# A decoder layer on one core: VectorE instead of GpSimd normalises blocks 2 and 3 in the middle of the expert stage, and their turns, logits and routing stand one or two units earlier

## The chip, the cores and the metric

The kernel runs on one core of a Trainium2 chip. The time is device microseconds (us) of one launch, and lower is better. Engines are named as in the profile: PE (TensorE matmuls), DVE (VectorE), ACT (ScalarE), POOL (GpSimd), SP (SyncE, which starts transfers).

## The reference, cut to what matters

The input is 16 rows of 128 tokens with 256 features. Three sublayers follow one another, each with a residual sum and a layer norm: a selective state-space mixer, a cross attention, and a mixture of experts (8 routed experts, 2 chosen for each token, and a shared one).

```python
def _layernorm(x, axis=-1, eps=1e-05):
    m = jnp.mean(x, axis=axis, keepdims=True)
    v = jnp.var(x, axis=axis, keepdims=True)
    return (x - m) / jnp.sqrt(v + eps)

scores = jax.nn.sigmoid((xt @ gate.T).astype(jnp.float32))
_, sel = jax.lax.top_k(scores + expert_bias[None, :], TOP_K)
...
h = jax.nn.silu(xb @ w1e.T) * (xb @ w3e.T)
oe = (h @ w2e.T).astype(routed.dtype)
...
x = _layernorm(x + _L0_attn_ref(x, L0_attn_W_in, ...), axis=-1)
x = _layernorm(x + _L0_xattn_ref(x, ctx_512, ctx_512), axis=-1)
x = _layernorm(x + _L0_ffn_ref(x, L0_ffn_gate, L0_ffn_expert_bias, ...), axis=-1)
```

## The kernel before

The tokens lie in `acc` (128 partitions, 16 batch rows, 256 features). Four batch rows make a **block**; there are blocks 0 to 3. The change lies in the last stage, the experts, which begins while the attention of the last rows still runs.

Each engine has its own written order of instructions, and semaphores tie them together. The expert stage walks through the list `users`: 32 **units** (`u`, half of the experts for one batch row, so that units 0 to 15 are blocks 0 and 1, and units 16 to 31 blocks 2 and 3) and four shared steps S0 to S3, one for each block. S1 stands behind unit 3, S2 behind unit 11, S3 behind unit 19. For one unit the work goes round the engines like this:

- PE `expert_up(u)`: four matmuls, two for `w_up` and two for `w_gate`, into two PSUM banks (L1661).
- ACT `silu_unit(u)`: four activations (L1301). DVE `gate_unit(u)`: four products into `hid` (L1461).
- PE `turn_hidden(u)`: four transposes (L1668), which wait for DVE's products of that unit. In PE's order they stand behind `expert_up(u+1)`. ACT `evac_hidden(u)` copies them out (L1307).
- PE `down(u)`: the matmuls into the output bank (L1687; for an even unit three more of the shared expert, L1683). In PE's order it stands behind `turn_hidden(u+1)`. After two units DVE adds the row (`add_row`, L1467), and after four it takes the moments for the last norm (L1472, L1477, L1480).

A shared step is twelve matmuls on PE (`shared_up`, L1647), one activation (L1293), one product on DVE (`gate_shared`, L1451), and a split in two float16 parts on POOL (`split_hidden`, L1164 and L1166).

Before a block can be used in this stage, its rows must pass the second layer norm (moments on DVE, an inverse root on POOL (L1132), the normalisation itself), then be transposed by PE (`turn_x`, L1620, two steps of eight transposes for a block in all), be copied out by ACT (L1259), and be split and cast by POOL (`split_x`, L1158 and L1160, and `cast_x`, L1179). The router follows: `logits` on PE (L1628), a copy on ACT (L1263), `turn_logits` on PE (L1635), tanh on ACT (L1267), and on DVE the steps `bias_scores`, `find_best`, `take_best`, `find_best`, `take_best`, `set_weights` (L1397 to L1417), small instructions that each wait for the one before. Unit 16 is the first that needs the second half's weights. The table `asides` says behind which unit the turns (`("x", i)`), the logits and their transposes of blocks 2 and 3 stand, on PE and on ACT; a chain of `if` in DVE's loop says behind which unit the norm and routing steps stand. The last layer norm's rows are normalised by POOL too (`finish`, L1171 and L1175).

DVE normalises blocks 0 and 1 here (`norm_part` with parts 3 and 4, L1760), and all blocks of the first layer norm in the mixer stage. Blocks 2 and 3 are normalised by POOL in `normalise_block` (L1185).

Of the kernel before, what the change touches and what calls it, by code (L numbers as in the profile page):

```python
# [15 lines left out]
ALU = mybir.AluOpType  # L16
# [9 lines left out]
KT = DM // P  # L26
# [4 lines left out]
TB = 4  # L31
TOK = BATCH // TB * L
NB = BATCH // TB
# [8 lines left out]
def makers(nc, ctx):  # L42

    names = {}

    def sb(name, shape, dt):
        return ctx.enter_context(nc.sbuf_tensor(name, shape, dt))

    def ps(name, shape, dt=F32):
        return ctx.enter_context(nc.psum_tensor(name, shape, dt))  # L50

    def sem(name):
        if name not in names:
            names[name] = ctx.enter_context(nc.semaphore(name))
        return names[name]

    return sb, ps, sem
# [886 lines left out]
def attention_and_experts(nc, io, acc, moments, heads, small, w_up, w_gate, w_down):  # L944
# [7 lines left out]
    with ExitStack() as ctx:  # L952
        sb, ps, sem = makers(nc, ctx)
# [6 lines left out]
        mean_var, rstd, expo = moments  # L960
# [64 lines left out]


        users = ["S0"] + list(range(4)) + ["S1"] + list(range(4, 12)) + ["S2"] + list(range(12, 20)) + ["S3"] + list(range(20, UNITS))
        asides = {4: [("x", 4), ("x", 5)], 8: [("x", 6), ("x", 7)], 9: [("logits", 1), ("turned", 1)]}
        turns = []
        for u in range(UNITS):  # L1030
            turns += [("hidden", u - 1)] * (u > 0) + asides.get(u, [])
# [76 lines left out]
        def _(pool):  # L1108
# [14 lines left out]
            def add_heads(b, t):  # L1123
                pool.wait_ge(sem("att"), 2 * b + t + 2)
                x = acc[:, bass.ds(b, 1), t * P:t * P + P]
                nc.gpsimd.tensor_tensor(x, x, att[:, t].unsqueeze(1), ALU.add).then_inc(sem("x_add"), 1)  # L1126

            def inverse_root(t):

                pool.wait_ge(sem("ln_var"), t + 1)  # L1130
                r = rstd[:, t * NB:t * NB + NB]
                nc.gpsimd.tensor_tensor(r, r, expo[:, 0:NB], ALU.pow).then_inc(sem("ln_rstd"), 1)  # L1132
# [23 lines left out]
            def split_x(t):  # L1156
                pool.wait_ge(sem("xt"), KT * t + KT)
                nc.gpsimd.tensor_copy(x_parts[:, 0, :, t, :], xt[:, :, t, :]).then_inc(sem("x_split"), 1)  # L1158
                pool.wait_ge(sem("x_split"), 2 * t + 1)
                nc.gpsimd.tensor_tensor(x_parts[:, 1, :, t, :], xt[:, :, t, :], x_parts[:, 0, :, t, :], ALU.subtract).then_inc(sem("x_split"), 1)  # L1160

            def split_hidden(t):
                pool.wait_ge(sem("shared_hid"), t + 1)
                nc.gpsimd.tensor_copy(hid_parts[:, 0, t], hid_s[:, t % 2]).then_inc(sem("hid_hi"), 1)  # L1164
                pool.wait_ge(sem("hid_hi"), t + 1)
                nc.gpsimd.tensor_tensor(hid_parts[:, 1, t], hid_s[:, t % 2], hid_parts[:, 0, t], ALU.subtract).then_inc(sem("hid_lo"), 1)  # L1166

            def finish(i):
                r = rstd3[:, finals[i][0]:finals[i][-1] + 1]
                pool.wait_ge(sem("ln3_var"), i + 1)  # L1170
                nc.gpsimd.tensor_tensor(r, r, expo[:, 0:len(finals[i])], ALU.pow).then_inc(sem("ln3_rstd"), 1)  # L1171
                if len(finals[i]) > 1:
                    pool.wait_ge(sem("ln3_rstd"), i + 1)
                    for b in finals[i]:
                        nc.gpsimd.tensor_scalar(acc[:, b], acc[:, b], mean_var3[:, b, 0:1], rstd3[:, b:b + 1], ALU.subtract, ALU.mult).then_inc(sem("final"), 1)  # L1175

            def cast_x(t):
                pool.wait_ge(sem("xt"), KT * t + KT)
                nc.gpsimd.tensor_copy(xb[:, :, t, :], xt[:, :, t, :]).then_inc(sem("xb"), 1)  # L1179

            def normalise_block(t):
                pool.wait_ge(sem("ln_mean"), t + 1)
                pool.wait_ge(sem("ln_rstd"), t + 1)
                for b in range(NB * t, NB * t + NB):
                    nc.gpsimd.tensor_scalar(acc[:, b], acc[:, b], mean_var[:, b, 0:1], rstd[:, b:b + 1], ALU.subtract, ALU.mult).then_inc(sem("pool_x"), 1)  # L1185

            add_heads(BATCH - 3, 0)
            add_heads(BATCH - 3, 1)
            inverse_root(0)
# [7 lines left out]
            add_heads(BATCH - 1, 1)  # L1197
            split_hidden(0)
            split_x(1)
            normalise_block(2)  # L1200
            split_hidden(1)
            cast_x(1)
            inverse_root(3)
            normalise_block(3)
            split_x(2)
            cast_x(2)
            finish(0)
            finish(1)
            split_hidden(2)
            split_x(3)  # L1210
            cast_x(3)
            finish(2)
            finish(3)
            split_hidden(3)
# [110 lines left out]
        def _(dve):  # L1325
# [57 lines left out]
            def routed(ins):  # L1383

                steps[0] += 1
                ins.then_inc(sem("route"), 1)
                dve.wait_ge(sem("route"), steps[0])
# [3 lines left out]
            def blocks(half):  # L1391
                return slice(HALF * half, HALF * half + HALF)

            def bias_scores(half):
                r = blocks(half)
                dve.wait_ge(sem("score"), half + 1)
                routed(nc.vector.tensor_scalar(score[:, r], score[:, r], 0.5, 0.5, ALU.mult, ALU.add))  # L1397
                routed(nc.vector.tensor_tensor(biased[:, r], score[:, r], ebias[:].unsqueeze(1).broadcast_to(full), ALU.add))

            def find_best(half):  # L1400
                r = blocks(half)
                routed(nc.vector.tensor_reduce(best[:, r], biased[:, r], AX.X, ALU.max))
                routed(nc.vector.tensor_tensor(equal[:, r], biased[:, r], best[:, r].unsqueeze(2).broadcast_to(full), ALU.is_equal))

                routed(nc.vector.tensor_tensor(equal[:, r], equal[:, r], earlier[:].unsqueeze(1).broadcast_to(full), ALU.mult))

            def take_best(half, i):
                r = blocks(half)
                routed(nc.vector.tensor_reduce(nearest[:, r], equal[:, r], AX.X, ALU.max))
                routed(nc.vector.tensor_tensor(chosen[:, i, r], equal[:, r], nearest[:, r].unsqueeze(2).broadcast_to(full), ALU.is_equal))  # L1410
                if i == 0:
                    routed(nc.vector.scalar_tensor_tensor(out=biased[:, r], in0=chosen[:, 0, r], scalar=NEVER, in1=biased[:, r], op0=ALU.mult, op1=ALU.add))
# [6 lines left out]
            def norm(t, *parts):  # L1419
                if parts[0] == 0 and t == TB - 1:  # L1420
                    dve.wait_ge(sem("x_add"), 2 * BATCH + 1)
                for i in parts:
                    norm_part(nc, dve, sem, acc, stats, block_mv, mean_var, rstd, t, i)
# [41 lines left out]
            def add_row(b):  # L1465
                dve.wait_ge(sem("down_mm"), 2 * b + 2)
                nc.vector.tensor_tensor(acc[:, b], po[b % 2][:, 0:DM], acc[:, b], ALU.add).then_inc(sem("row_add"), 1)  # L1467
# [28 lines left out]
            for u in users[1:]:  # L1496
                if isinstance(u, str):
                    gate_shared(int(u[1]))
                    continue
                gate_unit(u)  # L1500
                if u in (1, 2):
                    norm(TB - 1, *((0,), (1, 2))[u - 1])
                if u == 10:
                    bias_scores(1)
                elif u in (11, 13):
                    find_best(1)
                elif u in (12, 14):
                    take_best(1, (u - 12) // 2)
                elif u == 15:
                    set_weights(1)  # L1510
                b, odd = divmod(u - 3, 2)
                if b >= 0 and not odd:
                    add_row(b)
                    if b % 2 == 1:
                        final_stats(b // 2)
                elif b > 0 and b % 2 == 1:
                    final_aggr(b // 2)
# [10 lines left out]
        def _(pe):  # L1528
# [161 lines left out]
            b = BATCH - 2  # L1690
# [11 lines left out]
            b = BATCH - 1  # L1702
# [28 lines left out]
            for u in users[1:]:  # L1731
                if isinstance(u, str):
                    shared_up(int(u[1]), 0)
                    shared_up(int(u[1]), 1)
                    continue
                expert_up(u)
                if u >= 1:
                    turn_hidden(u - 1)
                if u >= 2:
                    down(u - 2)  # L1740
                for what, i in asides.get(u, []):
                    turn_free(pe, what, i)
                    if what == "x":
                        pe.wait_ge(sem("pool_x"), NB * (i // KT - 1))
                    {"x": turn_x, "logits": logits, "turned": turn_logits}[what](i, turn_bank(what, i))
            turn_hidden(UNITS - 1)
            down(UNITS - 2)
# [119 lines left out]
```

## Time and profile before

| | us |
|---|---|
| median of 3 runs | 766.42 (766.18 to 767.46) |
| the profiled execution's own time | 771.25 |
| its span, from the first to the last instruction | 769.4 |
| PE busy | 734.7 |
| DVE busy | 578.6 |
| ACT busy | 451.4 |
| POOL busy | 385.4 |

The span is what the trace shows; the execution's own time is 1.85 us longer. The expert stage takes the span from about 684 us to the end. Times in the rows below are counted from the start of the span. In a timeline or chain row the first number is the start and the second the length, both in us; "x4" are four instructions in a row that the view has merged; square brackets give the idle time just before and what ended it.

### The profile page before, as it was taken

To read this page: it belongs to the slowest core of one execution; us is meant where nothing else is said; L and a number is where in the kernel's file an instruction comes from. 1 tells how busy PE (TensorE), PEld (TensorE's weight loads), DVE (VectorE), ACT (ScalarE), POOL (GpSimd) and SP (SyncE) were. 2 spreads that over 40 slices of the span, in tenths; PEclk is the share of its full clock that TensorE was granted. 3 is DMA by queue.
4 is the path that set the end of the run, shared out by engine and by line. 5 is a ranking of instruction groups with operands and counts; after the bars stand their busy time and mean duration, and the time that the engine had idled before them with its cause. 6 is when DMAs were issued, how large, how long until landed. Compare 5 with 4: busy or idle time off the path is not lost. (4 is left out here: it accounts for less than half of the span.)

```text
span 769.4 us, 17375 instructions
## 1 busy us (share of the span) xinstructions
PE 734.7 (95%) x5929; PEld 407.0 (53%) x5938; DVE 578.6 (75%) x1134; ACT 451.4 (59%) x885; POOL 385.4 (50%) x439
## 2 busy tenths in 40 slices
PE   8899999999999999999999999999689999989797
PEld 3456565555655556555565655556423444335464
DVE  5568768687676767858677688887588889986777
ACT  7735446654444764444476453555537788877576
POOL 2858427473362655435357783554303321359744
PEclk9999999999999999999999999999969999999999
DMA  6565433115522242631313323340032000000001
GB/s 204 175 198 175 94 55 55 63 48 107 175 56 55 55 98 49 156 94 55 82 45 90 85 70 76 70 90 13 10 128 83 19 23 23 23 1 2 29 29 56
DMA packets 34299, 57.92 MB, mean 75 GB/s; under 512 B 7056, under 2 KB 11920, under 8 KB 33680
## 3 DMA queue, kind: packets, MB, share of 16 engines
q1 hardware_dynamic: 33680, 57.08, 28.0%
q8 instruction: 23, 0.38, 0.2%
q10 hardware_dynamic: 576, 0.31, 0.1%
q14 instruction: 20, 0.16, 0.1%
HBM read 54.10 MB, written 2.36 MB: 73 GB/s over the span
## 5 line engine op out<-in xcount | busy, mean ns | idle before, releaser
L285 POOL TENSOR_TENSOR cum_rows<-cum_rows,cum_t 128x512 f32<-128x512 f32 x128 | 136.5, 1076 | 197.7 <-DMA cum_rows<-cum_scratch 197.7
L788 PE MATMUL pring<-xt_hi,w_hi 128*128 (+1 forms) x576 | 172.5, 381 | 0.0
L788 PE MATMUL pring<-xt_lo,w_hi 128*128 (+1 forms) x576 | 171.9, 380 | 0.0
L788 PE MATMUL pring<-xt_hi,w_lo 128*128 (+1 forms) x576 | 171.5, 379 | 0.0
L650 DVE TENSOR_TENSOR bt<-pring,bt 128x512 f16<-128x512 f32 x128 | 88.1, 688 | 73.4 <-ACT bt L442 73.3
L442 ACT CAST bt<-pring 128x512 f16<-128x512 f32 x128 | 74.6, 583 | 115.3 <-PE pring L788 115.2
L654 DVE TENSOR_TENSOR ct<-pring,ct 128x512 f16<-128x512 f32 x128 | 88.2, 689 | 54.5 <-ACT ct L446 54.2
L830 PEld LDWEIGHTS pscore<-ct,bt 128*128 128x128 f16 x1536 | 96.6, 98 | 34.4 <-issue 6.2
L830 PE MATMUL pscore<-ct,bt 128*128 128x128 f16 x1536 | 107.2, 220 | 3.8 <-issue 2.2
L446 ACT CAST ct<-pring 128x512 f16<-128x512 f32 x128 | 74.8, 585 | 52.4 <-PE pring L788 52.2
L1336 DVE TENSOR_REDUCE mx<-bank_at 128x4 f32<-128x512 f32 x128 | 83.5, 689 | 14.3 <-PE bank_at L1544 13.2
L788 PEld LDWEIGHTS pring<-xt_lo,w_hi 128*128 128x128 f16 x576 | 56.6, 98 | 68.6 <-issue 1.1
L788 PEld LDWEIGHTS pring<-xt_hi,w_lo 128*128 128x128 f16 x576 | 56.5, 98 | 68.3 <-issue 0.7
L622 DVE TENSOR_TENSOR mt<-pscore,cum_rows 128x512 f32<-128x512 f32 x128 | 87.0, 681 | 0.9 <-ACT cum_rows L436 0.9
L436 ACT ACTIVATE cum_rows<-cum_rows 128x512 f32<-128x512 f32 x128 | 81.0, 634 | 0.7 <-POOL cum_rows L296 0.7
L296 POOL TENSOR_SCALAR_AFFINE_SELECT cum_rows<-cum_rows 128x512 f32<-128x512 f32 x128 | 81.1, 645 | 0.0
L1232 ACT ACTIVATE probs<-bank_at 128x512 f32<-128x512 f32 x128 | 68.5, 599 | 14.2 <-PE bank_at L1553 12.6
L788 PEld LDWEIGHTS pring<-xt_hi,w_hi 128*128 128x128 f16 x576 | 50.7, 98 | 42.5 <-issue 7.8
L266 POOL TENSOR_TENSOR w_lo<-w_raw,w_hi 128x512 f16<-128x512 f32 x34 | 41.5, 1240 | 26.7 <-ACT w_raw L408 26.7
L1544 PE MATMUL bank_at<-k_rows,q_rows 128*128 128x512 f16 x128 | 48.8, 416 | 5.5 <-DVE mx L1336 3.9
L1126 POOL TENSOR_TENSOR acc<-acc,att 128x128 f32<-128x128 f32 (+1 forms) x32 | 15.0, 470 | 76.5 <-DVE att L1349 76.5
L1461 DVE SCALAR_TENSOR_TENSOR hid<-bank_at,weight,act_s 128x128 bf16<-128x128 f32 x128 | 35.9, 343 | 11.7 <-PE bank_at L1661 6.5
(157 smaller groups left out, 983.1 us busy)
## 6 DMA issues: line engine op xcount, KB each, us to landing
cum_rows<-cum_scratch SPq DMA_DIRECT2D x32, 1024.0 KB, 8.0
w_raw<-in_w_in SPq DMA_DIRECT2D x35, 256.0 KB, 6.8
q_rows<-in_xt SPq DMA_DIRECT2D x4, 512.0 KB, 11.0
acc<-in_x SPq DMA_DIRECT2D x1, 2048.0 KB, 7.9
vals<-in_vals SPq DMA_DIRECT2D x16, 128.0 KB, 2.0
out<-acc SPq DMA_DIRECT2D x7, 256.0 KB, 2.1
w_raw_e<-in_w_up SPq DMA_DIRECT2D x1, 1024.0 KB, 5.0
w_raw_e<-in_w_gate SPq DMA_DIRECT2D x1, 1024.0 KB, 7.0
```

Of the source, the lines that this page charges most:

```text
L285: nc.gpsimd.tensor_tensor(rows[:, par, :, q], rows[:, par, :, q], own, ALU.subtract).then_inc(sem("since"), 1)
L296: nc.gpsimd.affine_select(rows[:, par, :, q], rows[:, par, :, q], [[0, NB], [1, L]], ALU.is_ge, never, base=0, channel_multiplier=-1).then ...
L436: nc.scalar.activation(rows[:, par, :, e % 4], rows[:, par, :, e % 4], ACT.Exp).then_inc(sem("decay_exp"), 1)
L442: nc.scalar.copy(bt[:, s % 2, 0], bank[f"B{s}"][:]).then_inc(sem("b_hi"), 1)
L446: nc.scalar.copy(ct[:, s % 2, 0], bank[f"C{s}"][:]).then_inc(sem("c_hi"), 1)
L622: nc.vector.tensor_tensor(mt[:, par, s % 4].rearrange("p (b n) -> p b n", b=NB), pscore[(s + 1) % 2][:].rearrange("p (b n) -> p b n", b=NB ...
L650: nc.vector.tensor_tensor(bt[:, s % 2, 1], bank[f"B{s}"][:], bt[:, s % 2, 0], ALU.subtract).then_inc(sem("b_evac"), 1)
L654: nc.vector.tensor_tensor(ct[:, s % 2, 1], bank[f"C{s}"][:], ct[:, s % 2, 0], ALU.subtract).then_inc(sem("c_evac"), 1)
L788: mm = nc.tensor.matmul(bank[name][:], w[:, c, k, cols], x[:, k, bass.ds(n % TB, 1), :].rearrange("p o n -> p (o n)"), start=(i == 0), sto ...
L830: mm = nc.tensor.matmul(pscore[(s + 1) % 2][:, cols], bt[:, s % 2, pb, cols], ct[:, s % 2, pc, cols], start=(i == 0), stop=(i == 2))
L1232: nc.scalar.activation(probs[:, i], ring_bank("scores", 8 * b + i)[:], ACT.Exp, scale=float(8.0 ** -0.5)).then_inc(sem("probs"), 1)
L1336: nc.vector.tensor_reduce(mx[:, slot, :, i], banks[i % len(banks)][:].rearrange("p (k n) -> p k n", k=4), AX.X, ALU.max).then_inc(sem("max ...
```

## The change

`normalise_block` is deleted. DVE does its work with the same `norm_part` as for blocks 0 and 1: block 2 behind the products of unit 1, block 3 behind those of unit 5. The moments of block 3 go from units 1 and 2 to units 2 and 3. The turns of block 2 go from unit 4 to unit 3 (so ahead of S1), those of block 3 from unit 8 to unit 6, the logits from unit 9 to 7, their transposes from 9 to 8. The routing steps go from units 10 to 15 to units 9 to 14. On POOL the order of what is left is changed: `cast_x(1)` and the inverse root of block 3 ahead of `split_hidden(1)`, and the split and the cast of block 3 ahead of `split_hidden(2)`, with `finish(0)` and `finish(1)` around them. PE's turns now wait for DVE's semaphore `ln_x`.

```diff
-        asides = {4: [("x", 4), ("x", 5)], 8: [("x", 6), ("x", 7)], 9: [("logits", 1), ("turned", 1)]}
+        asides = {3: [("x", 4), ("x", 5)], 6: [("x", 6), ("x", 7)], 7: [("logits", 1)], 8: [("turned", 1)]}
...
-            def normalise_block(t):
-                pool.wait_ge(sem("ln_mean"), t + 1)
-                pool.wait_ge(sem("ln_rstd"), t + 1)
-                for b in range(NB * t, NB * t + NB):
-                    nc.gpsimd.tensor_scalar(acc[:, b], acc[:, b], mean_var[:, b, 0:1], rstd[:, b:b + 1], ALU.subtract, ALU.mult).then_inc(sem("pool_x"), 1)
...
             split_x(1)
-            normalise_block(2)
-            split_hidden(1)
             cast_x(1)
             inverse_root(3)
-            normalise_block(3)
+            split_hidden(1)
             split_x(2)
             cast_x(2)
             finish(0)
+            split_x(3)
             finish(1)
+            cast_x(3)
             split_hidden(2)
-            split_x(3)
-            cast_x(3)
             finish(2)
...
-                if u in (1, 2):
-                    norm(TB - 1, *((0,), (1, 2))[u - 1])
-                if u == 10:
+                if u == 1:
+                    norm(2, 3, 4)
+                elif u in (2, 3):
+                    norm(3, *((0,), (1, 2))[u - 2])
+                elif u == 5:
+                    norm(3, 3, 4)
+                elif u == 9:
                     bias_scores(1)
+                elif u in (10, 12):
+                    find_best(1)
                 elif u in (11, 13):
-                    find_best(1)
-                elif u in (12, 14):
-                    take_best(1, (u - 12) // 2)
-                elif u == 15:
+                    take_best(1, (u - 11) // 2)
+                elif u == 14:
                     set_weights(1)
...
-                        pe.wait_ge(sem("pool_x"), NB * (i // KT - 1))
+                        pe.wait_ge(sem("ln_x"), NB * (i // KT + 1))
```

In the changed program the lines behind the deleted function have other numbers: what was L1461 is L1453, L1451 is L1443, L1467 is L1459, L1472 is L1464, L1760 is L1756, L1769 is L1765.

DVE's order from the products of units 0 and 1 (the row with x8) to those of unit 3 and the first `add_row`, before:

```order
L1461 SCALAR_TENSOR_TENSOR hid<-bank_at,weight,act_s 128x128 x8
L1769 BN_STATS stats<-acc 128x6 x4
L1461 SCALAR_TENSOR_TENSOR hid<-bank_at,weight,act_s 128x128 x4
L1774 BN_AGGR block_mv<-stats 128x2 x4
L1777 TENSOR_SCALAR rstd<-block_mv 128x4
L1778 TENSOR_SCALAR mean_var<-block_mv 128x4
L1461 SCALAR_TENSOR_TENSOR hid<-bank_at,weight,act_s 128x128 x4
L1467 TENSOR_TENSOR acc<-bank_at,acc 128x256
```

DVE's order at the same place in the changed program, and on to the products of unit 6:

```order
L1453 SCALAR_TENSOR_TENSOR hid<-bank_at,weight,act_s 128x128 x8
L1756 TENSOR_SCALAR acc<-acc,mean_var,rstd 128x256 x4
L1453 SCALAR_TENSOR_TENSOR hid<-bank_at,weight,act_s 128x128 x4
L1765 BN_STATS stats<-acc 128x6 x4
L1453 SCALAR_TENSOR_TENSOR hid<-bank_at,weight,act_s 128x128 x4
...
L1443 SCALAR_TENSOR_TENSOR hid_s<-bank_at,act_s 128x512
L1453 SCALAR_TENSOR_TENSOR hid<-bank_at,weight,act_s 128x128 x8
L1756 TENSOR_SCALAR acc<-acc,mean_var,rstd 128x256 x4
L1459 TENSOR_TENSOR acc<-bank_at,acc 128x256
L1464 BN_STATS stats<-acc 128x6 x2
L1453 SCALAR_TENSOR_TENSOR hid<-bank_at,weight,act_s 128x128 x4
```

Four normalising instructions stand where the four BN_STATS of block 3 stood, these stand one unit later, and four more stand between the products of units 5 and 6.

POOL's order from the split of the hidden part of S0 on, before (L1158 and L1160 are `split_x`, L1185 is `normalise_block`):

```order
L1166 TENSOR_TENSOR hid_parts<-hid_s,hid_parts 128x512
L1158 CAST w_raw_e<-xt_ex 128x2x512
L1160 TENSOR_TENSOR w_raw_e<-xt_ex,w_raw_e 128x2x512
L1185 TENSOR_SCALAR acc<-acc,mean_var,rstd 128x256 x4
L1164 CAST hid_parts<-hid_s 128x512
L1166 TENSOR_TENSOR hid_parts<-hid_s,hid_parts 128x512
L1179 CAST xb_ex<-xt_ex 128x2x512
L1132 TENSOR_TENSOR rstd<-rstd,expo 128x4
L1185 TENSOR_SCALAR acc<-acc,mean_var,rstd 128x256 x4
L1158 CAST w_raw_e<-xt_ex 128x2x512
L1160 TENSOR_TENSOR w_raw_e<-xt_ex,w_raw_e 128x2x512
L1179 CAST xb_ex<-xt_ex 128x2x512
```

The same place in the changed program:

```order
L1166 TENSOR_TENSOR hid_parts<-hid_s,hid_parts 128x512
L1158 CAST w_raw_e<-xt_ex 128x2x512
L1160 TENSOR_TENSOR w_raw_e<-xt_ex,w_raw_e 128x2x512
L1179 CAST xb_ex<-xt_ex 128x2x512
L1132 TENSOR_TENSOR rstd<-rstd,expo 128x4
L1164 CAST hid_parts<-hid_s 128x512
L1166 TENSOR_TENSOR hid_parts<-hid_s,hid_parts 128x512
L1158 CAST w_raw_e<-xt_ex 128x2x512
L1160 TENSOR_TENSOR w_raw_e<-xt_ex,w_raw_e 128x2x512
L1179 CAST xb_ex<-xt_ex 128x2x512
```

The two groups of four TENSOR_SCALAR are gone, and the casts and splits have moved up behind one another.

## Rows read from the trace of the kernel before

**Rows 1.** The page, part 1: busy time of each engine.

```profile
PE 734.7 (95%) x5929; PEld 407.0 (53%) x5938; DVE 578.6 (75%) x1134; ACT 451.4 (59%) x885; POOL 385.4 (50%) x439
```

**Rows 2.** The chain that ended last: start, length, engine, tile, line.

```profile
694.75 4.83 POOL acc L1185 x4
...
703.54 4.86 POOL acc L1185 x4
```

**Rows 3.** Timeline of PE, units 2 to 16: waits and the turns of blocks.

```profile
694.34 0.40 PE L1668 MATMUL bank_at<-ident_b,hid 128*128 128x128 bf16 x4 [0.31 <-DVE hid L1461]
...
695.01 2.75 PE L1647 MATMUL bank_at<-w_raw_e,s_up_parts 128*128 128x512 f16 x12
...
699.73 1.06 PE L1620 MATMUL bank_at<-ident,acc 128*128 128x128 f32 x8
...
708.53 1.06 PE L1620 MATMUL bank_at<-ident,acc 128*128 128x128 f32 x8 [0.65 <-POOL acc L1185]
...
713.73 0.43 PE L1635 MATMUL bank_at<-ident,lg 64*128 64x64 f32 x4 [0.77 <-ACT lg L1263]
...
725.17 0.40 PE L1668 MATMUL bank_at<-ident_b,hid 128*128 128x128 bf16 x4 [0.69 <-DVE hid L1461]
...
729.47 0.40 PE L1668 MATMUL bank_at<-ident_b,hid 128*128 128x128 bf16 x4 [2.28 <-DVE hid L1461]
```

**Rows 4.** Timeline of DVE from 691 us on.

```profile
691.86 1.40 DVE L1769 BATCH_NORM_STATS2 stats<-acc 128x6 f32<-128x256 f32 x4
693.17 1.11 DVE L1461 SCALAR_TENSOR_TENSOR hid<-bank_at,weight,act_s 128x128 bf16<-128x128 f32 x4
...
702.92 0.42 DVE L1467 TENSOR_TENSOR acc<-bank_at,acc 128x256 f32<-128x256 f32 x1
...
726.19 0.95 DVE L1405 TENSOR_TENSOR equal<-equal,earlier 128x64 f32<-128x64 f32 x1
```

**Rows 5.** Timeline of POOL from 691 us on.

```profile
691.50 1.03 POOL L1158 CAST w_raw_e<-xt_ex 128x1024 f16<-128x1024 f32 x1
692.62 2.13 POOL L1160 TENSOR_TENSOR w_raw_e<-xt_ex,w_raw_e 128x1024 f16<-128x1024 f32 x1
...
699.54 0.61 POOL L1164 CAST hid_parts<-hid_s 128x512 f16<-128x512 f32 x1
700.24 1.16 POOL L1166 TENSOR_TENSOR hid_parts<-hid_s,hid_parts 128x512 f16<-128x512 f32 x1
...
726.01 1.04 POOL L1179 CAST xb_ex<-xt_ex 128x1024 bf16<-128x1024 f32 x1
```

**Rows 6.** DVE's normalising instruction in the mixer stage: two pairs by the timeline.

```profile
473.03 0.73 DVE L1760 TENSOR_SCALAR acc<-acc,mean_var,rstd  x2
...
506.58 1.94 DVE L1760 TENSOR_SCALAR acc<-acc,mean_var,rstd  x2
```

**Rows 7.** POOL beside the second pair of rows 6, by the timeline.

```profile
506.27 2.10 POOL L285 TENSOR_TENSOR cum_rows<-cum_rows,cum_t 128x512 f32<-128x512 f32 x2 [1.67 <-DMA cum_rows<-cum_scratch]
```

**Rows 8.** Line L1760 alone, in a narrow window: duration in ns min/median/max, start.

```profile
L1760 DVE TENSOR_SCALAR acc<-acc,mean_var,rstd x1: 887/887/887, 506.6 to 506.6; - x1
```

**Rows 9.** Three stretches: length, busy time of each engine, granted clock (1.00 is full).

```profile
687.63:689.70 2.07, 0.16 (x1) 0.00 (x1) 1.90 (x8) 0.62 (x3) 0.04 (x1) 1.00 0.01 4
726.16:729.70 3.54, 1.26 (x10) 0.53 (x8) 3.40 (x10) 1.17 (x5) 0.90 (x1) 1.00 0.01 2
730.90:734.00 3.10, 2.88 (x14) 1.77 (x14) 2.42 (x9) 1.62 (x5) 2.70 (x3) 0.50 0.00 0
```

**Rows 10.** Timeline of PE without waits, units 20 and 21.

```profile
742.27 0.39 PE L1668 MATMUL bank_at<-ident_b,hid 128*128 128x128 bf16 x4
742.49 0.49 PE L1683 MATMUL bank_at<-s_down_parts,hid_parts 128*128 128x256 f16 x3
...
743.25 0.59 PE L1661 MATMUL bank_at<-w_up,xb_ex 128*128 128x512 bf16 x2
...
744.12 0.39 PE L1668 MATMUL bank_at<-ident_b,hid 128*128 128x128 bf16 x4
```

## The prediction, made before the changed kernel ran

> **What bounds the kernel now.** I read the page first: PE is busy for 95% of the span, DVE for 75%, POOL for 50% [rows 1]. A mean says little of one stage, so next the chain of waits, in the expert stage: it runs through POOL twice, for the 4.83 and 4.86 us in which `normalise_block` works on blocks 2 and 3 [rows 2]. Then PE's timeline, for what this costs [rows 3]. PE reaches the turns of block 3 and waits 0.65 us for POOL; the logits' transposes wait 0.77 for ACT's copy; `turn_hidden` waits 0.69 and 2.28 for DVE, which there has the routing steps between the units' products. Start to start these waits are some 0.16 longer than the brackets, because a matmul's end is modelled (the first is 0.8, the last two 0.9 and 2.4). Behind the last one the granted clock is 0.50, with 2.88 us of PE work in 3.10 us [rows 9]: at full clock that work takes half, so 1.4 us are lost. Elsewhere in this stage PE goes through without waits [rows 10], and there its work alone sets the time: `expert_up` 0.87 (743.25 to 744.12), `turn_hidden` 0.22, `down` of an even unit 0.76, of an odd one 0.44 (from 694.34 to S1 at 695.01, less 0.22) [rows 3, 10]. So what counts is PE's waits between unit 1 and unit 19, and the change moves nearly all of them.
>
> **What the routing steps wait for.** One of them, a product of two small SBUF tensors, took 0.95 us from 726.19 on, and ended at 727.14; POOL's cast beside it ran from 726.01 to 727.05 [rows 4, 5]. Such steps elsewhere take about 0.22. Three more are lengthened in the same way there. DVE is held until POOL's instruction ends. Does this hold for the normalising instruction as well, which has only one large operand? In the mixer stage two of them take 0.73 us with POOL idle, and 1.94 us beside two POOL instructions that run from 506.27 to 508.37 [rows 6, 7]. The first of the two began at 506.58 and took 887 ns, to 507.47 [rows 8]; POOL's first instruction ended at about 507.32 (half of 2.10). The second ended at 508.52, again 0.15 behind POOL's second. So one normalising instruction gets through for each POOL instruction, and ends 0.15 us behind it. BN_STATS, which stood at this place, was not held: four took 1.40 us beside POOL's cast and split [rows 4, 5].
>
> The Trainium skill (SBUF — State Buffer, "Who interferes with whom") says that VectorE and GpSimd share a pair of ports as an exclusive lock, that an instruction with at most one SBUF input contends only in a 2-port mode, and VectorE: DVE Perf Modes ("Mode 2×_2P") that this mode gives two results per cycle. By its duration alone (two in 0.73 us, as slow per element as BN_STATS) the instruction is in no such mode, and by that reading it would not be held: that is the second rival below, 762.4. The rows of the mixer stage speak against that reading, and I go by them.
>
> **Block 2 on DVE (behind unit 1).** DVE is free at 691.86, as before; nothing ahead of it changes. POOL's cast runs to 692.53, its split from 692.62 to 694.75, and now `cast_x(1)` follows at once, 1.04 us (the length of the same cast in rows 5), to 695.8 [rows 5]. By the rule of rows 6 to 8 the four instructions end at 692.7, 694.9, 695.9 and 696.3. Before, the products of unit 2 began at 693.17; now at 696.2: 3.0 us later. POOL's next instruction, the inverse root of block 3, waits for DVE itself and holds nobody. PE at that time has only `turn_hidden(2)` to do, which follows DVE directly: from 694.34 to 697.3, **+3.0**. Behind it everything on PE, S1 too, moves by as much. The moments of block 3, 1.4 us one unit later, lie beside PE's turns and S1 (0.9 and 2.6 us): nothing. Two waits of about 0.3 us go (ahead of the turns of block 2, which began at 699.73, and of `turn_hidden(6)`): **-0.6**.
>
> **Block 3 on DVE (behind unit 5).** Counted from the end of S1 on PE: `gate_shared(1)` is done 0.8 later, POOL's `split_hidden(1)` (0.61 and 1.16) ends at 2.7, the cast at 3.8, the split at 6.0, `cast_x(2)` at 7.0 [rows 5]. DVE comes to block 3 at 4.0 (PE's unit 4 takes 0.87 + 0.22 + 0.76 = 1.86, DVE's products of unit 5 begin 1.13 behind `expert_up(5)` and take 1.04). The split has just begun. So the four end at 6.1, 7.1, 7.5 and 7.8. With S1's end at 701.5 that is 709.3. PE comes to the turns at 706.8 and waits 2.6; before it waited 0.8: **+1.8**. DVE then owes `add_row` (0.42) and two moments (0.7) before the products of unit 6, so `turn_hidden(6)` waits **+0.4** [rows 4]. The logits and their transposes now stand one unit apart, so ACT's copy is hidden: **-0.8** [rows 3].
>
> **Routing one unit earlier.** Of before, PE's 0.9 + 2.4 + 1.4 (clock) + 0.2 = 4.9 us go. In their place I find, with DVE's own lengths and POOL's new order: `turn_hidden(10)` 0.65 (DVE has the bias step, a row and two moments ahead of it), `turn_hidden(13)` 1.0 (`find_best` beside `split_hidden(2)`, which costs it 1.1), `turn_hidden(14)` 0.75, `turn_hidden(15)` 0.4, together 2.8. The weights are ready a unit earlier, and unit 16 does not wait. **-4.9 + 2.8 = -2.1**.
>
> **The clock.** The new wait at `turn_hidden(2)` is 3.5 us long (693.9 to 697.3). Before, a wait of 2.4 us with another of 0.9 shortly ahead was followed by clock 0.50; one of 2.07 us was not [rows 9]. The new one is longer than both, so I take a stretch at half clock, over work that waits for nothing (turns, S1). It would lose at most the 1.4 of before, and less where it begins during the wait: **+1.2**.
>
> Sum: 3.0 - 0.6 + 1.8 + 0.4 - 0.8 - 2.1 = +1.7, and with the clock +2.9. The profiled execution takes 771.25 us (a span of 769.4 and 1.85 around it) and would take 774.2; it lies 4.8 above the median of 766.42, which I move by the same 2.9: **769.3**. POOL's saved 9.7 us are worth nothing in themselves: behind S3 POOL waits for DVE.
>
> **Rivals.**
> - *The clock stays up* after the new wait. For it: the wait may fall so that activity on both sides keeps the clock, as at 687.63. Against: its length. +1.7: 768.1.
> - *DVE is not held* (the side of faster). Place: the four normalising instructions behind units 1 and 5. Then they take 1.4 us as BN_STATS did, `turn_hidden(2)` stays at 694.3, the turns of block 2 run in the shadow of nothing and move 0.9 us ahead of S1, block 3 is ready 0.2 us behind PE. Unit 10 begins 1.8 us earlier, routing gives 2.1 to 2.3: -4.0, 762.4. It decides if each normalising instruction ends before POOL's instruction beside it. Against it stand rows 6 to 8; for it, that POOL has a gap of 0.1 us between cast and split, in which several might slip through.
> - *Held, but routing recovers more*: the 2.8 us of waits that I find in units 10 to 15 rest on DVE's lengths in a row, and vanish if the steps fit into its gaps. +2.9 - 2.8 = +0.1, and without the clock loss -1.1: 765.3 to 766.5.
> - *The clock falls a second time*, after the wait of 2.6 us at the turns of block 3: +4.1, 770.5.
>
> **Numbers.** A measurement of this kernel can tell about 0.2% (1.5 us) from no change. Held with one clock loss 0.45 (slower 0.42, same 0.03); clock stays 0.17 (same 0.09, slower 0.08); not held 0.17 (faster); routing recovers more 0.13 (faster 0.07, same 0.06); second clock loss 0.08 (slower). Sum: faster 0.24, same 0.18, slower 0.58. The likeliest case by itself gives 767.8 to 771.0 (its four waits are each worth some 0.5 either way). The range takes in all but the case "not held" and a tail above: 764.2 to 772.4.
>
> **What the new profile would show.** Right: the four normalising instructions behind unit 1 busy for about 4.4 us and those behind unit 5 for about 3.8, against 1.4 free; PE waits for DVE's product ahead of `turn_hidden(2)` about 3.3 us, and ahead of the second pair of turns about 2.5 us, then by DVE instead of POOL; clock 0.50 in some 3 us around S1; routing steps near 0.22 us each but for two beside `split_hidden(2)`; no wait ahead of the logits' transposes; S3 begins 2 to 4 us later than before. Wrong: four normalising instructions in 1.4 to 2 us (then not held), or S3 earlier than before. The size fails if PE's waits in units 10 to 15 are far from 2.8.

## The result and the profile after

The changed kernel takes 770.45 us (median of 10 runs, 769.05 to 775.54), the kernel before 767.61 us in 10 runs on the same chips. The ratio is 1.0041 with a 95% interval of 1.0021 to 1.0061: 1.6 to 4.7 us slower, 3.1 at the ratio itself. One run of the kernel before, of 1264.09 us at a mean granted clock of 0.557, is counted nowhere below.

The span of the one profiled execution says something else at first sight: 767.5 us after, 769.4 before. That is not the change. S0, the first shared step, begins at 680.49 us after and at 684.16 before, and up to there both kernels do the same work. Two runs below, k4_pool_order and m2_turns, are alike up to there as well, and S0 begins at 684.02 in one and at 678.92 in the other. So all profiles below are compared from S0's first matmul to the end of the span, here called **the stage**: 769.4 - 684.16 = 85.2 us before, 767.5 - 680.49 = 87.0 us after. The stage is 1.8 us longer.

Busy times of the engines after, from the page; they answer to [rows 1]:

```profile
PE 732.6 (95%) x5938; PEld 405.4 (53%) x5938; DVE 583.3 (76%) x1142; ACT 451.7 (59%) x885; POOL 376.1 (49%) x431
```

POOL does 9.3 us less and DVE 4.7 us more, though the eight instructions that moved would take DVE only some 2.8. The timeline of DVE in the changed kernel, for [rows 4]:

```profile
688.18 4.40 DVE L1756 TENSOR_SCALAR acc<-acc,mean_var,rstd 128x256 f32<-128x256 f32 x4
...
701.85 3.80 DVE L1756 TENSOR_SCALAR acc<-acc,mean_var,rstd 128x256 f32<-128x256 f32 x4
...
723.84 1.22 DVE L1397 TENSOR_TENSOR equal<-equal,earlier 128x64 f32<-128x64 f32 x1
```

And that of POOL beside it, for [rows 5]:

```profile
687.82 1.03 POOL L1158 CAST w_raw_e<-xt_ex 128x1024 f16<-128x1024 f32 x1
688.94 2.12 POOL L1160 TENSOR_TENSOR w_raw_e<-xt_ex,w_raw_e 128x1024 f16<-128x1024 f32 x1
691.00 1.10 POOL L1179 CAST xb_ex<-xt_ex 128x1024 bf16<-128x1024 f32 x1
...
701.69 2.13 POOL L1160 TENSOR_TENSOR w_raw_e<-xt_ex,w_raw_e 128x1024 f16<-128x1024 f32 x1
703.76 1.10 POOL L1179 CAST xb_ex<-xt_ex 128x1024 bf16<-128x1024 f32 x1
```

Four normalising instructions that could take 1.4 us take 4.40: they begin within POOL's cast, last over its split and its second cast, and end 0.5 us behind that; the second four take 3.80, over a split and a cast. The timeline of PE, for [rows 3], shows who waits:

```profile
693.67 0.40 PE L1664 MATMUL bank_at<-ident_b,hid 128*128 128x128 bf16 x4 [1.83 <-DVE hid L1453]
...
705.79 1.06 PE L1616 MATMUL bank_at<-ident,acc 128*128 128x128 f32 x8 [2.58 <-DVE acc L1756]
...
717.76 0.40 PE L1664 MATMUL bank_at<-ident_b,hid 128*128 128x128 bf16 x4 [0.55 <-DVE hid L1453]
...
726.27 0.40 PE L1664 MATMUL bank_at<-ident_b,hid 128*128 128x128 bf16 x4 [0.84 <-DVE hid L1453]
...
728.93 0.40 PE L1664 MATMUL bank_at<-ident_b,hid 128*128 128x128 bf16 x4 [0.63 <-DVE hid L1453]
```

`turn_hidden(2)` comes 13.2 us behind S0 (693.67 - 680.49), before 10.2. The turns of block 3 wait 2.58 us, now for DVE, before 0.65 for POOL. The logits' transposes (at 712.42) wait no more. In units 10 to 15 PE waits 0.55, 0.84 and 0.63 for the products of units 10, 13 and 14, before 0.69 and 2.28 (units 13 and 14) with a stretch at half clock behind. For the size of a wait the starts say more than the brackets: without a wait `turn_hidden` begins 0.43 us behind the `w_gate` matmuls ahead of it (743.69 to 744.12 in the trace before), and what is over that is 0.71, 1.01, 0.80 and, for unit 15, which has no bracket, 0.29: 2.8 together.

### The profile page after: what moved, and what is told of

The parts are those of the page before. It is cut to its first block and busy times, and to the rows that moved or that the text cites. A ratio compares the mean times of both kernels' runs of the same rounds, so it can differ in the third digit from the quotient of the medians.

```text
span 767.5 us, 17386 instructions
## 1 busy us (share of the span) xinstructions
PE 732.6 (95%) x5938; PEld 405.4 (53%) x5938; DVE 583.3 (76%) x1142; ACT 451.7 (59%) x885; POOL 376.1 (49%) x431
## 5 line engine op out<-in xcount | busy, mean ns | idle before, releaser
L1293 ACT ACTIVATE act_s<-bank_at,weight 128x128 f32<-128x128 f32 x128 | 36.6, 370 | 11.9 <-PE bank_at L1657 8.9
```

## The experiments

The stage of each kernel is read in the same way as above, and S0 to S1, S1 to S2 and S2 to S3 are the distances of the shared steps' first matmuls on PE:

```
kernel            S0-S1  S1-S2  S2-S3  S3-end  stage  ratio to before (95%)
before            10.85  22.47  21.33  30.6    85.2   1
changed           14.74  23.20  18.44  30.6    87.0   1.0041 (1.0021 to 1.0061)
k1_accum          13.13  21.33  18.42  30.6    83.5   0.9988 (0.9966 to 1.0010)
k2_casts_later    14.04  23.02  18.43  30.6    86.1   1.0020 (1.0002 to 1.0038)
k3_block2_only    13.86  21.42  20.46  31.0    86.7   1.0044 (1.0023 to 1.0064)
k4_pool_order     10.85  22.43  18.69  30.6    82.6   0.9972 (0.9951 to 0.9994)
m2_turns          10.85  21.02  18.66  30.7    81.2   0.9967 (0.9940 to 0.9995)
m1_all            11.84  20.74  17.80  30.6    81.0   0.9923 (0.9898 to 0.9948)
r_routing_back    16.01  23.86  18.93  30.6    89.4   1.0062 (1.0039 to 1.0085)
```

Each ratio is to runs of the kernel before that were made beside it: 33 for k1 to k4, 22 for the last three. S3 to the end is the same in all but one (31.0). What differs lies between S0 and S3.

**k1_accum: the same normalising work in a form that is not held.**

```diff
+        return nc.vector.tensor_scalar(acc[:, b], acc[:, b], mean_var[:, b, 0:1], rstd[:, b:b + 1], ALU.subtract, ALU.mult, accum_out=total[:, b:b + 1])
...
-            normalise_row(nc, acc, mean_var, rstd, t * NB + b).then_inc(sem("ln_x"), 1)
+            normalise_row(nc, acc, mean_var, rstd, t * NB + b, total).then_inc(sem("ln_x"), 1)
```

In this form the second operation serves the accumulator, so blocks 2 and 3 don't come out normalised as in the reference; the number of elements read and written is the same.

> The changed kernel, but the eight normalising instructions of blocks 2 and 3 also write out their accumulator (a sum into a scratch column that nobody reads), the form that the Trainium skill (SBUF — State Buffer, "Who interferes with whom") excludes from the 2-port modes. Theory 1 (DVE is held because this instruction takes the pair of ports that it shares with GpSimd): in this form it is not held; the two groups of four take 1.4 to 2.2 us each in place of 4.4 and 3.8, PE's waits at turn_hidden(2) and at the second pair of turns shrink to under 0.8 us each, and the stage from S0's first matmul to the end, 87.0 us in the profile of the changed kernel, comes down by 4 to 6 us, to about 82; the time falls to about 3 to 4 us below that of the kernel before. Rival (any instruction on DVE that reads and writes large SBUF tiles is held, whatever its mode): the groups stay at 4.4 and 3.8 us or get longer by the accumulator reads, and the stage stays at 87.

Measured: DVE's timeline of the first group (each instruction is followed by a read of the accumulator of 0.08 us; the other three pairs of the group and the whole second group read alike, 0.53 or 0.54 us each and 0.46 from one start to the next):

```profile
689.18 0.53 DVE L1758 TENSOR_SCALAR_CACHE_REDUCE acc<-acc,mean_var,rstd 128x256 f32<-128x256 f32 x1
```

POOL beside it:

```profile
688.81 1.04 POOL L1159 CAST w_raw_e<-xt_ex 128x1024 f16<-128x1024 f32 x1
689.93 2.13 POOL L1161 TENSOR_TENSOR w_raw_e<-xt_ex,w_raw_e 128x1024 f16<-128x1024 f32 x1
```

PE:

```profile
703.29 1.06 PE L1617 MATMUL bank_at<-ident,acc 128*128 128x128 f32 x8 [0.70 <-DVE acc L1758]
```

The group is over in 1.9 us, across the same cast and split, and nothing is held. `turn_hidden(2)` has no wait at all, the turns of block 3 wait 0.70 instead of 2.58. The stage falls by 3.5 us to 83.5; that is less than the 4 to 6 expected, because in this execution the granted clock was 0.51 from 688.5 to 691.9, with PE busy throughout: from `expert_up(2)` to the next `expert_up` it took 3.51 us, before 2.03, so 1.5 were lost. The kernel is as fast as the one before (0.9988, the interval holds 1), not 3 to 4 us faster as expected. So the hold is shown to hang on the form of DVE's instruction, not on the size of its tiles: the rival falls. The Trainium skill (SBUF — State Buffer, "Who interferes with whom") has it that the form that also writes its accumulator can't enter a 2-port mode and so doesn't contend; this trace agrees, with 0.46 us from one start to the next beside POOL's cast and split.

**k2_casts_later: one POOL instruction fewer beside each group.**

```diff
             split_x(1)
-            cast_x(1)
             inverse_root(3)
+            cast_x(1)
             split_hidden(1)
             split_x(2)
-            cast_x(2)
             finish(0)
+            cast_x(2)
```

> The changed kernel, but POOL does cast_x(1) behind inverse_root(3) and cast_x(2) behind finish(0), so that one POOL instruction fewer runs beside each group of four. Theory 1 (one normalising instruction gets through for each POOL instruction): block 2's group takes about 3.7 instead of 4.4 us, block 3's about 3.1 instead of 3.8; both PE waits shrink by 0.7; the stage goes from 87.0 to about 85.6 us, the time to about that of the kernel before (+0.3 us). Rival (the length comes from DVE's own instruction or from the two-operand split alone, not from the cast): groups unchanged, stage 87.0.

Measured, DVE's timeline:

```profile
689.07 3.68 DVE L1756 TENSOR_SCALAR acc<-acc,mean_var,rstd 128x256 f32<-128x256 f32 x4
...
702.02 3.09 DVE L1756 TENSOR_SCALAR acc<-acc,mean_var,rstd 128x256 f32<-128x256 f32 x4
```

4.40 becomes 3.68 and 3.80 becomes 3.09, each 0.7 less, as one instruction through for each of POOL's wants it. The stage gives back 0.9 of the 1.4: the first 0.7 in full (S0 to S1), the second mostly not, since POOL's later order now holds the bias step (0.72 us, before 0.19) and the wait at the products of unit 10 goes from 0.55 to 1.08. The ratio of 1.0020 (1.5 us, 0.2 to 2.9) is still slower than before, by more than the 0.3 expected, though the interval only just leaves out no change.

**k3_block2_only: one part of the change alone.** The kernel before, with block 2 normalised by DVE behind unit 1 and the moments of block 3 a unit later:

```diff
-            normalise_block(2)
-            split_hidden(1)
             cast_x(1)
             inverse_root(3)
+            split_hidden(1)
...
-                if u in (1, 2):
-                    norm(TB - 1, *((0,), (1, 2))[u - 1])
+                if u == 1:
+                    norm(2, 3, 4)
+                elif u in (2, 3):
+                    norm(3, *((0,), (1, 2))[u - 2])
...
-                        pe.wait_ge(sem("pool_x"), NB * (i // KT - 1))
+                        pe.wait_ge(sem("ln_x" if i < 6 else "pool_x"), 3 * NB if i < 6 else NB)
```

> The kernel before with one part of the change: only block 2 is normalised by DVE (behind unit 1, moments of block 3 a unit later); turns, logits, routing and block 3 on POOL as before. Theory 1: the group takes 4.4 us, turn_hidden(2) comes 3.0 us later counted from S0; the small wait at the turns of block 2 (0.3) and PE's wait for block 3 (0.8) go, because POOL is free earlier; routing waits stay. Stage from 85.3 to about 86.9 us, time about 1.6 us above the kernel before. Rival (POOL's saved 4.9 us are what counts, since POOL's normalising was on the chain of waits): stage 84.5 or less, faster.

Measured, the group on DVE:

```profile
686.50 4.40 DVE L1761 TENSOR_SCALAR acc<-acc,mean_var,rstd 128x256 f32<-128x256 f32 x4
```

And PE, at `turn_hidden(2)` and at `turn_hidden(14)`:

```profile
691.99 0.40 PE L1669 MATMUL bank_at<-ident_b,hid 128*128 128x128 bf16 x4 [3.33 <-DVE hid L1460]
...
726.06 0.40 PE L1669 MATMUL bank_at<-ident_b,hid 128*128 128x128 bf16 x4 [2.28 <-DVE hid L1460]
```

The stretch behind the second of them (length, busy time of the engines, clock):

```profile
726.06:729.46 3.40, 3.10 (x25) 2.08 (x27) 3.06 (x14) 1.52 (x5) 2.40 (x3) 1.00 0.00 0
```

4.40 us again, and S0 to S1 is 3.0 us longer than before. The wait for block 3 is gone (S1 to S2 is 1.05 shorter). POOL's 4.8 us, though they stood in the chain of waits [rows 2], bought those 1.05.

S2 to S3 is 0.87 shorter too, and the change to block 2 has no part in that: PE's waits of 0.69 and 2.28 are the same as before, but here the clock stays at 1.00 behind them, where before it fell to half. In its place PE waits 0.24 and 0.18 for DVE further on, so the stretch at half clock of the kernel before cost 0.9 net. The stage of 86.7 meets the 86.9 expected only with the help of those 0.87.

The profile is also the kindest of the 11 runs: 767.31 us is the fastest of them, at a mean granted clock of 0.989. One other run has 0.989 (769.84 us); the nine others have 0.981 to 0.985 and take 769.61 to 773.76. The ratio of 1.0044 puts this half of the change at 3.4 us (1.8 to 4.9), not the 1.6 expected, about as much as the whole change costs (1.0041).

**k4_pool_order: only POOL's order, in the kernel before.**

```diff
             cast_x(2)
+            split_x(3)
+            cast_x(3)
             finish(0)
             finish(1)
             split_hidden(2)
-            split_x(3)
-            cast_x(3)
```

> The kernel before with POOL's order alone changed: split_x(3) and cast_x(3) straight behind cast_x(2), ahead of finish(0), so that neither runs beside the routing steps of units 12 to 14. Theory 1 (the routing waits of before, 0.9 and 2.4 us on PE and the clock loss behind them, come from DVE being held by POOL's split and casts): the routing steps take 0.22 to 0.3 us each but for one or two, the two PE waits shrink to 0.3 and 0.5 us, the clock stays up, stage from 85.3 to about 82 us, time 3 us below the kernel before. Rival (DVE has too much work between the products of units 13 to 15 anyway, so a routing step earlier is what is needed): waits stay over 2 us together, stage 84.5 or more.

Measured, PE's timeline:

```profile
727.51 0.40 PE L1668 MATMUL bank_at<-ident_b,hid 128*128 128x128 bf16 x4 [1.38 <-DVE hid L1461]
```

The wait of 0.69 is gone, that of 2.28 is 1.38 (expected 0.5), and no stretch at half clock follows. S2 to S3 falls from 21.33 to 18.69, the stage to 82.6. So moving two calls in POOL's queue takes 2.6 us from this stretch, 0.9 of it the half-clock stretch (see k3_block2_only) and 1.8 the waits (20.46 to 18.69). The changed kernel takes 2.9 (18.44), but has a new wait of 0.7 for the products of unit 10 just ahead of S2: 2.2 net. The time is 2.1 us below that of the kernel before (0.5 to 3.8), 3 were expected. The rest of the wait is DVE's own load in units 13 to 15, where a row, its moments and `find_best` come together: here the rival is in part right, and m1_all below, where they are spread, has no such wait.

**r_routing_back: the routing steps undone.** The changed kernel with the steps at units 10 to 15 again:

```diff
-                elif u == 9:
+                elif u == 10:
                     bias_scores(1)
-                elif u in (10, 12):
+                elif u in (11, 13):
                     find_best(1)
-                elif u in (11, 13):
-                    take_best(1, (u - 11) // 2)
-                elif u == 14:
+                elif u in (12, 14):
+                    take_best(1, (u - 12) // 2)
+                elif u == 15:
                     set_weights(1)
```

> The changed kernel with one part undone: the routing steps of block 2 and 3 stand at units 10 to 15 again, as in the kernel before; norms on DVE, turns, logits and POOL's order as changed. Theory 1 (of the 4.9 us that the change takes from PE's waits behind unit 10, most comes from POOL's split and casts no longer running beside the steps, not from the unit earlier): stage 87.0 to 88.5 us, PE waits 1.5 us more in sum, in units 13 to 16. Rival (the unit earlier is what counts): the waits of the kernel before come back, stage 90 us or more.

Measured: S2 to S3 is 18.93, 0.5 us more than in the changed kernel, far from the 21.33 of before. But `turn_hidden(10)`, just ahead of S2, has no wait here: it begins 0.66 behind the `w_gate` matmuls (721.46 to 722.12), in the changed kernel 1.14 (716.62 to 717.76). That is 0.5 us less. So the earlier routing by itself is worth nothing: it moves half a microsecond of waiting from one side of S2 to the other. The stage is 89.4 all the same, over the 87.0 to 88.5 expected, and the granted clock says why. Two stretches (length, busy time of the engines, clock):

```profile
695.30:698.70 3.40, 2.60 (x15) 2.42 (x16) 3.37 (x15) 0.83 (x2) 0.00 (x0) 0.51 0.02 5
708.90:712.30 3.40, 2.58 (x10) 2.16 (x12) 2.89 (x12) 1.17 (x2) 0.36 (x1) 0.52 0.00 0
```

PE waits for DVE at `turn_hidden(2)` (3.33 us, to 696.10), and for the last 0.8 us of the wait and 2.6 behind it the clock is at half; it waits at the turns of block 3 (2.59 us, to 709.50), and the same happens. S0 to S1 is 1.3 us longer than in the changed kernel, though up to S1 the two programs are the same. From the turns of block 3 to the logits (709.50 to 713.45) PE takes 3.95 us, in the changed kernel 2.83: 1.1 lost. With the 0.0 net of the routing that is the whole difference of 2.4 between the stages.

**m2_turns and m1_all: a version that beats both.** POOL keeps the normalising. On POOL the work of block 3 stands straight behind that of block 2; the turns and logits move up by one unit; m1_all also spreads the routing steps.

```diff
-        asides = {4: [("x", 4), ("x", 5)], 8: [("x", 6), ("x", 7)], 9: [("logits", 1), ("turned", 1)]}
+        asides = {4: [("x", 4), ("x", 5)], 7: [("x", 6), ("x", 7)], 8: [("logits", 1)], 9: [("turned", 1)]}
...
             normalise_block(2)
-            split_hidden(1)
-            cast_x(1)
             inverse_root(3)
             normalise_block(3)
+            cast_x(1)
+            split_hidden(1)
             split_x(2)
             cast_x(2)
+            split_x(3)
+            cast_x(3)
             finish(0)
             finish(1)
             split_hidden(2)
-            split_x(3)
-            cast_x(3)
```

m1_all alone:

```diff
-                elif u in (11, 13):
+                elif u == 11:
                     find_best(1)
-                elif u in (12, 14):
-                    take_best(1, (u - 12) // 2)
+                    take_best(1, 0)
+                elif u == 12:
+                    find_best(1)
+                elif u == 14:
+                    take_best(1, 1)
```

(The wait that these two expectations place at `turn_hidden(15)` is that of unit 14.)

> As m1_all, but the routing steps stay where the kernel before has them (bias 10, find 11, take 12, find 13, take 14, set 15). Theory 1: the waits for block 3 and the logits go (1.5 us), the 1.4 us at turn_hidden(15) stays: stage about 81.2 us. Rival (DVE's lateness there only came from the logits being late): the wait at turn_hidden(15) goes too, and m1_all is no faster than this.

> The kernel before (POOL keeps both normalisations) with three reorderings: on POOL the inverse root and normalisation of block 3 straight behind those of block 2, and split and cast of block 3 ahead of finish(0); turns of block 3 behind unit 7, logits behind 8, their transposes behind 9; the routing steps spread as bias 10, find and take 11, find 12, take 14, set 15. Theory 1 (what costs is DVE work beside POOL's split, casts and two-operand instructions, and routing steps in units that also have a row and its moments): PE's waits of 0.6 and 0.8 us for block 3 and the logits go, the 1.4 us at turn_hidden(15) of the run k4_pool_order falls under 0.8; S0 to the end about 80.5 us against 85.3 before and 82.6 in k4_pool_order. Rival (the gain of moving turns and logits is eaten by a new wait of PE for POOL at unit 7, or unit 8 waits for cast_x(1)): a wait of 1 us or more at the turns or at expert_up(8), stage 82 us or more.

Measured in m2_turns, PE's timeline:

```profile
720.97 0.40 PE L1668 MATMUL bank_at<-ident_b,hid 128*128 128x128 bf16 x4 [1.18 <-DVE hid L1461]
```

and in m1_all, where the turns of block 3 have no wait and none behind them is above 0.23:

```profile
725.64 0.40 PE L1671 MATMUL bank_at<-ident_b,hid 128*128 128x128 bf16 x4 [0.23 <-DVE hid L1461]
```

The waits for block 3 and for the logits go in both (S1 to S2 from 22.43 in k4_pool_order to 21.02), and spreading the routing takes the last wait. m2_turns has a stage of 81.2 us, as expected (81.2). m1_all has 81.0 against 80.5 expected; in its execution the clock was at half from 688.7 to 692.1, and S0 to S1 is 11.84 there in place of 10.85. Without that it would be at 80.0. m1_all is the fastest kernel of the study: 0.9923 (0.9898 to 0.9948), 4.0 to 7.8 us faster than the kernel before. m2_turns is 0.4 to 4.6 us faster; its twelve runs are spread from 761.63 to 770.28 us.

## Why the prediction was right

**The forecast** was slower, 2.9 us above the kernel before. The ratio puts the change at 3.1 (1.6 to 4.7). The steps:

- *Block 2 on DVE, +3.0 at `turn_hidden(2)`*: measured 13.2 - 10.2 = +3.0, with the group at 4.40 us (forecast 4.4). k2 and k3 repeat it; k1 takes the hold away and the wait goes. The mechanism is shown.
- *Block 3, +1.8*: the group takes 3.80 (3.8), PE waits 2.58 (2.6) in place of 0.65. `turn_hidden(6)` behind it comes 0.3 late (+0.4).
- *Logits, -0.8*: no wait is left.
- *Routing, -4.9 + 2.8*: start to start the four waits are 0.71, 1.01, 0.80 and 0.29, 2.8 together, each within 0.11 of the one forecast (0.65, 1.0, 0.75, 0.4). S2 to S3 is 2.9 us shorter and the wait ahead of S2 0.7 longer, -2.2 for the -2.1 forecast. The size holds, the name does not: the heading of that step was "one unit earlier", and r_routing_back shows that the unit earlier gives nothing net; k4_pool_order shows that a new order on POOL alone gives 2.6. And of the 4.9, the 1.4 for the clock is what the profile of before has, not what its waits always cost: in k3_block2_only the same waits had no half-clock stretch behind them, and S2 to S3 was 0.9 shorter.
- *Sum without the clock, +1.7*: the stage grew by 1.8; S3 begins 1.7 us later than before counted from S0, a little under the 2 to 4 named as a sign.
- *The clock, +1.2*: in the profiled execution of the changed kernel the clock did not fall behind the new wait. It fell earlier, after the wait of 1.91 us that both kernels have ahead of unit 1:

```profile
687.60:691.00 3.40, 3.40 (x16) 1.99 (x15) 3.40 (x5) 2.31 (x7) 3.32 (x3) 0.51 0.00 0
```

There it cost nothing, because PE had to wait for DVE behind it anyway (1.83 us instead of 3.33 as in k3_block2_only). So the wait of about 3.3 us and the clock of 0.50 around S1, which the forecast named as signs, are not in this profile. In k3_block2_only the clock stayed up throughout the wait of 3.33 us, and in r_routing_back it fell at both waits and cost 1.3 and 1.1. So the step that took a stretch at half clock as given, because the wait is longer than one that had it, is too simple: the same wait does it in one execution and not in another. The 1.2 is the one term of the sum that the profile does not bear out, and without it the forecast of 1.7 would also lie within the measured 1.6 to 4.7; that 2.9 came so near 3.1 is in part luck.

The runs behind the medians have no trace of the stage, but each has the mean clock of its whole span, and that speaks for a loss of this kind in most of them. The ten of the changed kernel have 0.979 to 0.986 (mean 0.9844), the eleven of k3_block2_only 0.9843, and the 33 of the kernel before that were made beside k3_block2_only 0.9867. A stretch of 3.4 us at half clock lowers such a mean by 0.0022. A mean does not say where the clock was low, nor what it cost, so this is an argument and not shown.

**The rivals.** "DVE is not held" is refuted by the 4.40 and 3.80 us. Its estimate of -4.0 for that case can be set against k1_accum, where DVE indeed is not held: 3.5 us less than the changed kernel in the stage and 1.7 less than before, with 1.5 us lost at half clock in it. "Routing recovers more" did not come: 2.8 us of waits were left. Between "one clock loss", "the clock stays up" and "a second clock loss" one profile can't decide; r_routing_back shows an execution with the clock down at both waits.

**The absolute time** of 769.3 stands 1.15 under the median of 770.45, because the kernel before is itself at 767.61 in ten runs and not at the 766.42 of the three that were shown.

## What to carry to other kernels

Work that an idle-looking engine gives to a busy one is priced beside what the first will do instead: 4.8 us on POOL were cheap, 1.4 us on DVE became 4.4 as soon as POOL's casts and splits lay beside them. Before moving work between these two engines, look for a row in which DVE's instruction already runs beside POOL (here in another stage, with 1.94 in place of 0.73 us), and ask in which form it stands. Small steps with many waits can be cheapest to mend by the other engine's order: two calls moved in POOL's queue gave 2.6 us, where the whole change took 2.2 net from the same waits. Look on both sides of a mark before calling a wait gone: the earlier routing only moved half a microsecond across S2. And where the start of a stage shifts from run to run (S0 began between 678.80 and 684.16 us in nine profiles), compare stages from a fixed instruction on, and see whether the profiled run is a typical one of its kernel.

## What the runs showed of the hardware that was not expected

- POOL's own normalising instruction (TENSOR_SCALAR, 1.22 us, in `finish`) hardly holds DVE's steps with two SBUF operands: in the trace before, one of them took 0.31 us beside it and the next (the product of `equal` and `earlier`) 0.22, while beside POOL's TENSOR_TENSOR that same step took 1.22 in the changed kernel. Whether DVE's own normalising instruction would pass beside it as well, no run shows.
- DVE's bias step, a TENSOR_SCALAR of only 128x64, is held as well: 0.72 us in k2_casts_later and 0.83 in m2_turns, against 0.19 in the changed kernel.
- DVE's normalising instruction is held, and yet no faster than BN_STATS when free (0.73 us for two [rows 6], BN_STATS 1.40 for four [rows 4]); the accumulator form, never held, costs 0.46 from start to start.
- The clock fell behind a wait of PE of 1.91 us in three of nine profiles (changed, k1_accum, m1_all) and not in the other six, with the same program up to there. Behind waits of 0.69 and 2.28 us it fell in the kernel before and not in k3_block2_only; at one of 3.33 us it fell in r_routing_back and not in k3_block2_only.
